# Decoder layer: a group's four smallest score blocks share one PSUM bank, with one exponential, a subtraction and a sum

## The reference

```python
kqv = x @ Wqkv + bqkv                       # first third is q, second k, third v
scores = einsum('bsnh,btnh->bnst', k, q) / sqrt(32)
scores = triu(scores) - 10000 * tril(ones, k=-1)
attn = softmax(scores, axis=2)
out = einsum('bnkq,bknh->bqnh', attn, v).reshape(b, s, 512) @ Wo + bo
x = layernorm(x + out)
x = layernorm(x + wkv(w, u, k=x, v=ctx))    # a decaying recurrence over the 512 tokens
h = silu(x @ Wg.T) * (x @ Wu.T)             # 2048 wide, weights dequantised: (wq - 128) * scale
x = layernorm(x + h @ Wd.T)
```

## Time and profile before

| | |
|---|---|
| median of 3 runs | 708.04 us (707.57 to 708.64) |
| profiled execution, its own time | 711.66 us |
| its span | 709.9 us |
| mean granted TensorE clock | 0.989 |
| busy: PE, DVE, ACT, POOL | 671.4, 513.2, 496.1, 395.7 us |

### The profile page before, as it was taken

One profiled execution on the slowest core, in us unless ns is written; L12 is line 12 of the kernel. 1 busy time (PEld: TensorE's weight loads), 2 busy tenths in 40 slices (PEclk: granted clock), 3 DMA queues, 4 the chain that ended last, 5 costly groups with the idle time before them and its releaser, 6 DMA issues.

```text
span 709.9 us, 12525 instructions
## 1 busy us (share of the span) xinstructions
PE 671.4 (95%) x4290; PEld 380.8 (54%) x4290; DVE 513.2 (72%) x1220; ACT 496.1 (70%) x1143; POOL 395.7 (56%) x508
## 2 busy tenths in 40 slices
PE   8979999899988989799989999999999999999996
PEld 3435555445445545454445454544456797578845
DVE  4676767787888899989755569858777786655644
ACT  5798889789897879978787873384754855336620
POOL 6035735846999664864596654885771634103321
PEclk9999999999999999989999999999999999999999
DMA  7878944322332136460071002000001000000001
GB/s 239 249 218 235 217 145 135 98 75 79 124 102 78 38 85 163 120 143 16 8 120 60 1 0 75 16 31 0 1 1 44 17 1 2 30 31 1 1 16 45
DMA packets 45024, 54.33 MB, mean 77 GB/s; under 512 B 5921, under 2 KB 33825, under 8 KB 44961
## 3 DMA queue, kind: packets, MB, share of 16 engines
q1 hardware_dynamic: 41264, 46.85, 21.6%
q0 software_dynamic: 3264, 6.29, 5.4%
q10 hardware_dynamic: 432, 0.39, 0.2%
HBM read 45.00 MB, written 12.71 MB: 81 GB/s over the span
## 4 chain that ended last, share of the span: by engine, by line
PE 61%; DVE 13%; ACT 10%; POOL 5%; issue 5%; DMA 4%; SPq 1%; POOLq 0%; DVEq 0%; ACTq 0%
PE psb L1160 12%; PE psb L1133 8%; PE psb L996 6%; PE psb L1184 5%; PE psb L1182 5%; PE psb L1104 4%; PE psb L1072 4%; PE psb L1027 4%; DVE ee L1530 3%; PE psb L1039 3%; PE psb L1056 3%; DVE x L1607 2%; PE psb L1120 2%; PE psb L1083 2%; ACT L1330 1%
## 5 line engine op out<-in xcount | busy, mean ns | idle before, releaser
L1530 DVE CUSTOM_DVE_ANT_0 ee<-psb,mask,clip 128x512 f32<-128x512 f32 (+3 forms) x256 | 131.3, 542 | 24.9 <-PE psb L1039 22.3
L1278 ACT ACTIVATE ee<-ee,nm 128x512 f32<-128x512 f32 (+3 forms) x256 | 142.2, 560 | 1.4 <-DVE nm L1530 1.4
L1938 POOL TENSOR_TENSOR hl<-ring,hh 128x512 f16<-128x512 f32 x64 | 80.1, 1264 | 86.7 <-ACT hh L1414 57.3
L1288 ACT ACTIVATE ee<-psb 128x256 f32<-128x256 f32 (+1 forms) x192 | 94.6, 523 | 31.0 <-PE psb L1056 21.0
L1182 PE MATMUL psb<-wd,hh 128*128 128x512 f16 x240 | 91.0, 379 | 0.0
L1184 PE MATMUL psb<-wd,hl 128*128 128x512 f16 x240 | 91.0, 379 | 0.0
L1868 POOL TENSOR_SCALAR_AFFINE_SELECT ee<-ee 128x256 f32<-128x256 f32 x128 | 56.8, 452 | 60.7 <-ACT ee L1288 59.9
L1039 PE MATMUL psb<-ks,qs 128*128 128x512 f16 (+3 forms) x256 | 72.5, 305 | 8.3 <-DVE nm L1530 6.1
L1056 PE MATMUL psb<-qs,ks 128*128 128x128 f16 (+3 forms) x256 | 60.1, 306 | 9.6 <-ACT ee L1288 7.5
L996 PE MATMUL psb<-xh,wqk 128*128 128x512 f16 x240 | 61.8, 385 | 1.7 <-POOL xh L1830 1.2
L1885 POOL TENSOR_TENSOR rs<-ve,half 128x1 f32<-128x1 f32 (+1 forms) x24 | 20.5, 854 | 72.0 <-DVE ve L1599 71.7
(11 more groups left out here) (217 smaller groups left out, 1668.2 us busy)
## 6 DMA issues: line engine op xcount, KB each, us to landing
qs<-parts SPq DMA_DIRECT2D x48, 128.0 KB, 2.7
ks<-parts SPq DMA_DIRECT2D x45, 128.0 KB, 2.9
parts<-qhl SPq DMA_DIRECT2D x16, 256.0 KB, 2.2
parts<-khl SPq DMA_DIRECT2D x16, 256.0 KB, 2.2
x<-in_x SPq DMA_DIRECT2D x4, 1024.0 KB, 6.8
ct<-in_ctxT SPq DMA_DIRECT2D x4, 1024.0 KB, 5.1
out<-x SPq DMA_DIRECT2D x16, 256.0 KB, 2.0
xt<-in_xT SPq DMA_DIRECT2D x14, 256.0 KB, 3.4
```

Of the source, the lines that this page charges most:

```text
L1278: e.activation(dst, dst, ACT.Exp, bias=NM[:, n % 4, col:col + 1], scale=-1.0, accum_out=DEN[:, n % 4, col:col + 1]).then_inc(sem("exp"), 1)
L1288: e.activation(ET[H % ET_SLOTS][:, base:base + width], PSB[:, bank["turn", H, item], 0:width], ACT.Exp, scale=SC).then_inc(sem("et"), 1)
L1530: e.tensor_tensor_reduce(E[H % E_SLOTS][:, EOFF[i]:EOFF[i] + w], PSB[:, bank["score", H, i], 0:w], MASK[:, S - w:S], -SC, CLIP[:, i:i + 1] ...
L1938: e.tensor_tensor(HS[it][1][:], pair(b, it // 2)[:, it % 2, :] if b in SEVEN else ring(b, it)[1], HS[it][0][:], ALU.subtract).then_inc(sem ...
```

## The change

Scores of block i = 0 are 128 x 128 for each head. They leave `score`, `weigh` and `exp`, which now treat i = 3, 2, 1 alone, in the first three of a head's four slots. In their place stands `firsts(n)`, once a group, at slot FIRST_AT[n]: four matmuls into one general bank, 128 columns each. DVE takes the four maxima with the same instruction as before, written back into the bank (`weigh0`), and subtracts each head's maximum in one instruction over 512 columns (`less0`); ACT raises the whole bank in place, with no bias and no accumulator (`exp0`); DVE sums each head's 128 columns into den (`total0`), and the bank is free. `mq`, `emx` and the denominators wait for `weigh0` or `total0` as well.

Some copies out of PSUM go from ACT to DVE: `eb` of groups 1, 3, 8, 11 and 14, `vtake` of batch 1 (four), `mrow` of groups 1, 2, 3, 5 and 8. `oh` of group 8 goes from POOL to ACT. Nearly all tables of slots have new numbers, mostly by 0 to 3 slots; the diff shows those that are spoken of.

```diff
-EOFF = {0: 0, 1: 128, 2: 384, 3: 768}
+EOFF = {1: 0, 2: 256, 3: 640}
...
+SIGNAL = {"firsts": "score", "weigh0": "weigh", "less0": "weigh", "total0": "weigh", "exp0": "exp", "snap1": "snap", "snap5": "snap", "snap6": "snap", "c11": "summed", "c12": "summed", "c22": "summed"}
...
-QK_AT = {2: (12, 18), 3: (18, 25), 4: (37, 46), 5: (45, 53), 6: (70, 79), 7: (75, 84), 8: (103, 117), 9: (125,
-         132), 10: (134, 139), 11: (144, 150), 12: (169, 173), 13: (176, 198), 14: (205, 210), 15: (216, 224)}
...
+QK_AT = {2: (12, 19), 3: (19, 23), 4: (36, 45), 5: (44, 51), 6: (72, 79), 7: (77, 84), 8: (102, 118), 9: (125,
+         132), 10: (136, 139), 11: (143, 151), 12: (170, 173), 13: (176, 198), 14: (205, 212), 15: (217, 222)}
...
+FIRST_AT = {1: 20, 2: 32, 3: 43, 4: 65, 5: 79, 6: 95, 7: 115, 8: 127, 9: 142, 10: 158, 11: 174, 12: 190, 13: 207,
+            14: 223, 15: 238}
...
-WAIT = {'high': 1, 'low': 1, 'vtake': 2, 'r1': 2, 'norm': 6, 'exp': 4, 'eb': 0, 't1': 1, 't3': 0, 'oh': 2, 'ol':
-        2, 'ek': 1, 'scan_q': 2, 'scan_p': 12, 'seed': 6, 'refine': 8, 'divide': 13, 'r2': 1, 'x2h': 0, 'x2l': 0,
-        'expand': 0}
-WAIT_IN = {'r1': 1, 'norm': 3, 'ek': 0, 'scan_q': 0, 'scan_p': 9, 'seed': 10, 'refine': 3, 'divide': 6, 'r2': 0,
-           'x2h': 0, 'x2l': 0, 'norm2': 7}
...
+WAIT = {'weigh0': 0, 'exp0': 1, 'total0': 1, 'high': 1, 'low': 1, 'vtake': 2, 'r1': 2, 'norm': 6, 'exp': 4, 'eb':
+        0, 't1': 1, 't3': 1, 'oh': 2, 'ol': 2, 'ek': 1, 'scan_q': 2, 'scan_p': 13, 'seed': 6, 'refine': 8,
+        'divide': 13, 'r2': 1, 'x2h': 0, 'x2l': 0, 'expand': 3}
+WAIT_IN = {'r1': 0, 'norm': 4, 'ek': 0, 'scan_q': 0, 'scan_p': 16, 'seed': 15, 'refine': 3, 'divide': 6, 'r2': 0,
+           'x2h': 2, 'x2l': 0, 'norm2': 8}
...
-PIECE_AT = {'load_second': 31, 'small': 66, 'split_wo': 47, 'load_ds': 180}
...
+PIECE_AT = {'load_second': 34, 'small': 74, 'split_wo': 50, 'load_ds': 185}
...
-XLOAD = {1: (0, 2, 24, 29), 2: (49, 63, 83, 88), 3: (130, 136, 148, 164)}
-XSPLIT = {1: (20, 26, 34, 34), 2: (83, 85, 98, 98), 3: (148, 156, 158, 165)}
...
+XLOAD = {1: (3, 5, 26, 31), 2: (58, 75, 80, 85), 3: (143, 144, 153, 170)}
+XSPLIT = {1: (22, 27, 33, 36), 2: (82, 85, 91, 102), 3: (147, 155, 157, 166)}
...
-OH_POOL = (1, 1, 1, 1, 1, 1, 0, 0, 1, 1, 1, 1, 1, 1, 1, 0)
...
+OH_POOL = (1, 1, 1, 1, 1, 1, 0, 0, 0, 1, 1, 1, 1, 1, 1, 0)
...
+EB_DVE = (0, 1, 0, 1, 0, 0, 0, 0, 1, 0, 0, 1, 0, 0, 1, 0)
+VTAKE_DVE = (0, 1, 0, 0)
+MROW_DVE = (0, 1, 1, 1, 0, 1, 0, 0, 1, 0, 0, 0, 0, 0, 0, 0)
...
     "score": lambda H, i: ("weigh", H, i),
+    "firsts": lambda n: ("total0", n),
...
+    def firsts(n):
+        tt.unit("firsts", n)
+        add("firsts", n)
+        late(WAIT["weigh0"], lambda: first_max(n))
+
+    def first_max(n):
+        add("weigh0", n)
+        add("less0", n)
+        late(WAIT["exp0"], lambda: first_exp(n))
+
+    def first_exp(n):
+        add("exp0", n)
+        late(WAIT["total0"], lambda: add("total0", n))
 
...
-    for i in (3, 2, 1, 0):
+    for i in (3, 2, 1):
         score(0, i)
         weigh(0, i)
         tick()
+    firsts(0)
+    tick()
...
+    for n, slot in FIRST_AT.items():
+        at(slot, lambda n=n: firsts(n))
...
-            if H + 1 < NHG:
+            if H + 1 < NHG and k < 3:
...
+        def firsts(n):
+            emptied(("firsts", n))
+            pe.wait_ge(*by_stack(n, "q"))
+            pe.wait_ge(*by_stack(n, "k"))
+            pe.wait_ge(*by_made("rows"))
+            for h in range(4):
+                mm = e.matmul(PSB[:, bank["firsts", n], h * P:(h + 1) * P], heads(n, "q")[:, h, 0:P],
+                              heads(n, "k")[:, h, 0:P], start=True, stop=True)
+            mm.then_inc(sem("score"), 1)
+
...
+        def first_exp(n):
+            act.wait_ge(*by("less0", n))
+            block = PSB[:, bank["firsts", n], :]
+            e.activation(block, block, ACT.Exp, scale=-1.0).then_inc(sem("exp"), 1)
+
...
-            act.wait_ge(*by("weigh", 4 * n + 3, 0))
+            act.wait_ge(*by("weigh", 4 * n + 3, 1))
+            act.wait_ge(*by("weigh0", n))
...
-                dve.wait_ge(*by("exp", H - E_SLOTS, 0))
+                dve.wait_ge(*by("exp", H - E_SLOTS, 1))
...
+        def vtake(b, t):
+            dve.wait_ge(*by("v", b, t))
+            if b >= 2:
+                dve.wait_ge(*by("pv", 4 * b - 5))
+                dve.wait_ge(*by("sv", 4 * b - 5))
+            e.tensor_scalar(VV[:, b % 2, t, :], PSB[:, bank["v", b, t], :], 1.0 / WS, None, ALU.mult).then_inc(sem("vtake"), 1)
+
+        def eb(n):
+            dve.wait_ge(sem("spread0"), n + 1)
+            if n:
+                dve.wait_ge(*by("ol", n - 1))
+            e.tensor_scalar(EB[:], PSB[:, bank["spread", n, 0], :], 1.0, None, ALU.mult).then_inc(sem("eb"), 1)
+
+        def shift_rows(n):
+            dve.wait_ge(*by("mt", n))
+            if n:
+                dve.wait_ge(*by_mput(n - 1))
+            e.tensor_scalar(MROW[:], PSB[0:32, bank["mt", n], 0:P], 1.0, None, ALU.mult).then_inc(sem("mrow"), 1)
+
+        def first_max(n):
+            dve.wait_ge(*by("firsts", n))
+            dve.wait_ge(*by_consts())
+            for h in range(4):
+                block = PSB[:, bank["firsts", n], h * P:(h + 1) * P]
+                op = e.tensor_tensor_reduce(block, block, MASK[:, S - P:S], -SC, CLIP[:, 0:1], ALU.add, ALU.min,
+                                            NM[:, n % 4, 4 * h:4 * h + 1])
+            op.then_inc(sem("weigh"), 1)
+
+        def first_less(n):
+            block = PSB[:, bank["firsts", n], :].rearrange("p (h s) -> p h s", h=4)
+            least = NM[:, n % 4, :].rearrange("p (h i) -> p i h", h=4)[:, 0, :]
+            dve.wait_ge(*by("weigh0", n))
+            e.tensor_tensor(block, block, least.unsqueeze(2).broadcast_to([P, 4, P]), ALU.subtract).then_inc(sem("weigh"), 1)
+
+        def first_total(n):
+            block = PSB[:, bank["firsts", n], :].rearrange("p (h s) -> p h s", h=4)
+            sums = DEN[:, n % 4, :].rearrange("p (h i) -> p i h", h=4)[:, 0, :]
+            dve.wait_ge(*by("exp0", n))
+            e.tensor_reduce(sums, block, mybir.AxisListType.X, ALU.add).then_inc(sem("weigh"), 1)
+
...
-            dve.wait_ge(*by("weigh", 4 * n + 3, 0))
+            dve.wait_ge(*by("weigh", 4 * n + 3, 1))
+            dve.wait_ge(*by("weigh0", n))
...
-            pool.wait_ge(*by("exp", 4 * n + 3, 0))
+            pool.wait_ge(*by("exp", 4 * n + 3, 1))
+            pool.wait_ge(*by("total0", n))
```

More of the change, by code:

```diff
@@ L123 @@
+YT_AT = {0: (172, 179, 185, 191), 1: (1013, 1013, 1014, 1015), 2: (1025, 1025, 1026, 1030), 3: (1045, 1047, 1049,
+         1051)}
+X2_AT = {0: (222, 224, 229, 233), 1: (1018, 1018, 1018, 1018), 2: (1035, 1035, 1036, 1036), 3: (1055, 1055, 1055,
+         1056)}
+WO_IN = (3, 7, 12, 13)
+WD_AT = (258, 258, 258, 259)
+ZERO_IN = (1, 3, 4, 6, 8, 9, 11, 12, 12, 12, 13, 13, 13, 13, 15, 16)
+WS_AT = {1: (1016, 1018), 2: (1027, 1034), 3: (1019, 1028), 4: (1033, 1035)}
 WS_POOL = (0, 0, 0, 0)
@@ L1201, in _ @@
                 score(*a)
+            elif name == "firsts":
+                firsts(*a)
             elif name == "turn":
@@ L1436, in hh @@
             elif it >= 4:
-                act.wait_ge(*by("exp", NHG - 1, 0))
+                act.wait_ge(*by("exp", NHG - 1, 1))
             else:
@@ L1459, in _ @@
                     e.dma_start(*stacked(0, "k", r)).then_inc(sem("stackk0"), 16)
-            elif name == "vtake":
+            elif name == "vtake" and not VTAKE_DVE[a[0]]:
                 vtake(*a)
+            elif name == "exp0":
+                first_exp(*a)
             elif name == "exp":
@@ L1465, in _ @@
                 et(*a)
-            elif name == "mrow":
+            elif name == "mrow" and not MROW_DVE[a[0]]:
                 shift_rows(*a)
@@ L1469, in _ @@
                 emx(*a)
-            elif name == "eb":
+            elif name == "eb" and not EB_DVE[a[0]]:
                 eb(*a)
@@ L1747, in _ @@
                 weigh(*a)
+            elif name == "weigh0":
+                first_max(*a)
+            elif name == "less0":
+                first_less(*a)
+            elif name == "total0":
+                first_total(*a)
             elif name == "expand":
                 expand(*a)
+            elif name == "vtake" and VTAKE_DVE[a[0]]:
+                vtake(*a)
+            elif name == "eb" and EB_DVE[a[0]]:
+                eb(*a)
+            elif name == "mrow" and MROW_DVE[a[0]]:
+                shift_rows(*a)
             elif name == "mq":
```

61 lines of the change are left out of this document (26 added, 35 removed), and 18 rows, old and new, of the table TURN_AT.

## The result

Over 20 executions each, taken in turn, the changed kernel took 712.96 us in the median (709.21 to 716.03) and the kernel before 708.94 (707.12 to 711.66). The ratio is 1.0047, with a 95% interval of 1.0031 to 1.0063: 3.3 us slower (the medians differ by 4.0), where 2.4 us faster was forecast. A later comparison gave 1.0059 (1.0035 to 1.0084).

A forecast was written before the change was run, and what follows sets the result against it. The prediction took PE, busy 95%, as the bound, still waiting for ScalarE and VectorE in the attention part. Its terms summed to -2.4 us: 709.3 us against the profiled 711.66, 705.6 against the median 708.04; range 699.5 to 713.5.

The forecast's parts named there:

- the first term of its sum: PE's waits for ScalarE's exponentials of the turned scores, taken as 10 us, shrink with ScalarE's higher idle share: -4.4 us.
- both other signs: Outcomes besides faster by over 0.2% (chance 0.46): the same, 0.15, and slower, 0.39.
- ScalarE's relief: Over 16 groups, one wide exponential replaces four with their reads, and copies leave: ScalarE loses 34.7 us.
- VectorE's added load: A subtraction and a sum in each group, plus the moved copies: VectorE gains 29.6 us.
- Term 2: Before 240 us, PE's stalls ended by VectorE grow as VectorE's idle share falls from 24 to 14%: +3.6 us.
- term 3: Small score matmuls leave the three score banks; the longer rotation removes 40% of 8 us of waits for maxima: -3.2 us.
- Term 4: The two later clock dips follow PE stalls; one half of their 5.1 us goes: -2.5 us.
- Term 5: From 240 to 350 us, VectorE's added 8.3 us must fit 8.9 us of idle; half fits: +4.1 us.
- Term 6: Loads and ordering waits moved by some slots, taken at nothing; batch 1's x wait -1.2 to +3.9, tail -2 to +2 us.
- VectorE becomes the bound: None of VectorE's added 8.3 us fits its idle after 240 us: +5 us, 713 us; chance 0.32.
- The handover costs: Maxima, exponential and sum pass VectorE, ScalarE, VectorE one slot apart; waits or the held bank cost +3 us, 711; chance 0.07.

The follow-up runs named there:

- the kernel with light subtraction and sum: The changed kernel with the subtraction and the sum cut to one column a head in all groups, waits kept: ratio 1.0000 to the kernel before.
- the common maximum: Changed kernel with one 512-wide maximum for a row's four heads, no subtraction: 1.0005; versions at 1.0004 and 1.0025 also move group 3's first blocks to slot 46.

## Why the prediction was wrong

The step that failed is the first term of its sum, "Stalls that ACT ends: 10 us, scaled by its idle share before and after". It read PE's wait for ScalarE as a sign of ScalarE's average load. The kernel without the first exponentials shows that 22 us less on ScalarE are worth nothing to the old order: 7.5 us of waits became 6.3, and the time did not fall. The traces show the waits where some other step stands ahead of the exponential in ScalarE's order (7.2 of the 7.5 us, 9.4 of 9.8 after the change), and the third turn bank takes most of them away at the same load (9.8 to 2.8 us). Expected -4.4 us, found none, and the waits themselves went up by 2.3 us in the first pair of profiles and 3.3 in the second.

The measured 712.96 us lies inside the stated range of 699.5 to 713.5, which was made wide enough for both other signs; the sign of the forecast was wrong.

Point by point:
- **ScalarE's relief** was forecast as 34.7 us and came out as 20.2. The prices of single steps were right, the sum was not: an accumulator read lies over its exponential and over the next step, so a 128-wide exponential and its read are not 398 + 199 ns. In the kernel before:

```profile
40.27 0.39 ACT L1278 ACTIVATE ee<-ee,nm 128x128 f32<-128x128 f32 x1
40.56 0.19 ACT L1278 ACTIVATION_READ_ACCUMULATOR ee<-ee,nm 128x1 f32 x1
40.65 0.62 ACT L1255 ACTIVATE wqk<-stg 128x512 f16<-128x512 f32 x1
```

  The next instruction starts 0.38 us after the exponential did. Four of these are 1.5 us, not 2.39. By this the blocks would save 16 x (1.52 - 0.60) = 14.7 us. Measured are 15.6, by the run with the copies back (496.1 to 480.5 us); the copies save 4.6, where 6.0 was forecast. **VectorE's added load** was forecast as 29.6 and is 27.0 us, 21.1 of it the blocks' and 5.9 the copies'.
- **Term 2** (VectorE's waits before 240 us rise by 3.6) and **term 3** (the longer rotation, -3.2): the rotation was the stronger. The waits for the maxima went from 6.1 to 1.1 us, where the two terms together left them about unchanged. That the rotation does it is shown from two sides: the new tables with the old blocks have 10.7 us, and the change with two score banks 18.1. The mechanism was right and undersized.
- **Term 4** (a half of the later clock dips, -2.5): in the one profile the dip at 217 us went and that at 300 us shrank, 3.4 us back, and the one at 50 us took 1.7 us more. Over many executions the mean clock is the same, 0.989 and 0.990, so nothing of this term is to be seen. Its premise failed too: the kernel before, once more, had the same stalls without the dips, and no shorter span for it.
- **Term 5** (+4.1, VectorE after 240 us): the right kind of cost, too narrow a place. The subtraction and the sum in these five groups cost 1.3 to 2.2 us, in the eleven early ones 1.2 to 2.1 us, where none was put except through term 2. Cut in all groups they are the whole 3.3 us.
- **Term 6** (moved steps, at nothing): the wait for the mask grew from 0.6 to 3.4 us, and the waits for the stacked k from 1.2 to 2.9 us. In the kernel with light subtraction and sum they stand too (3.8 us for the mask, 2.3 for k) at 1.0000, so they may be paid for by the maxima's waits that went; no run takes them away alone. The wait for x that this term bounded at -1.2 to +3.9 us is gone from the list of the changed kernel.

The rival "VectorE becomes the bound" gave 713 us for a measured 712.96. Its sign is right; that the figures meet is luck, since it priced +5 us on 708 and the change is +3.3 on 708.9. Its mechanism is only half shown: work added to VectorE is the loss, but at 96%, under the 97% named as its point, and probably over both halves. And it is not VectorE's total load alone: the common maximum with the copies back has VectorE at 522.9 us and 1.0025, with the copies moved 530.7 us and 1.0004. "The handover costs" is refuted as far as slots go: one more between maxima and exponential gained nothing.

What stays open: with the load gone, the order still does not beat the kernel before (1.0000 to 1.0005), in spite of 5 us less waiting for maxima; and moving the copies back, which lightens VectorE further, gained nothing that is clear of noise (1.0039 for 1.0047, 1.0025 for 1.0004). Part of the time probably hangs on how the tables fit the durations for which they were made, and no run here separates that from load. A table made anew for the common maximum was not tried.

## What to carry to other kernels

A wait of PE for an engine does not say that the engine is overloaded. Look in the timeline at what that engine ran just before the step that released PE. If it stood idle until PE's result came, the wait is a round trip of the banks; if it came straight from another step, as in 11 of the 12 waits here, the wait is that step's place in the order, and a third bank may cover it. That the engine also waits for PE in sum doesn't tell them apart: ScalarE stood 21.0 us for these products before the change, 25.3 after, and 33.7 with the third bank. Price a transfer of work by what the receiving engine's queue delays; the giving engine's relief counts only if something waits for its load. And sum busy time from starts of instructions in a timeline, not from mean durations, where one instruction's record lies over the next.

## What was unexpected of the hardware

- Four maxima in a row written to PSUM took 353 ns each and their accumulator reads 140 ns, against 343 to SBUF and, for all widths before, some 81 ns (20.8 us over 256). A single 512-wide maximum in place (the common maximum) had a read of 141 ns too, so it is not that four follow each other.
- The in-place exponential over 512 columns of PSUM took 596 ns, the same as one from PSUM to SBUF at 594.
- The same stalls of PE, up to 2.22 us, came with a fall of the granted clock in one execution of the kernel before and without it in another (mean 0.989 and 0.994), and the spans were equal (709.9 and 709.8 us).
- Executions of the same kernel, one after the other, spread by 1% (709.21 to 716.03 us), with mean granted clocks of 0.986 to 0.995; the clock explains a part only (a span of 714.2 us came with 0.987, one of 713.2 with 0.986, but one of 712.1 with 0.992 and one of 709.0 with 0.988).
